# Two blocks of each Q head from exact codes, their scales applied inside Q's accumulator; a partition exchange by DMA; context rounding by an 8-bit store

## What is computed

```python
def _dequant(codes, scales):                       # codes 0..15, one scale per 128 rows and column
    w = codes.astype(jnp.float32) - 8.0
    return w * jnp.repeat(scales, GS, axis=0)      # GS = 128
q = hidden_states @ _dequant(q_codes, q_scales)    # 32 heads of 128; k, v: 8 heads
q = _rope(q); k = _rope(k)
attn = softmax(q @ k.T * HD ** -0.5 + causal_mask)
out = (attn @ v) @ _dequant(o_codes, o_scales)
def fake_quant(x, scale, zp):                      # for the context and for the normed x
    q = jnp.clip(jnp.round(x / scale + zp), 0.0, 255.0)
    return (q - zp) * scale
```

## Time and profile before

| | us |
|---|---|
| median of three runs (1077.76 to 1079.20) | 1079.08 |
| the profiled execution | 1078.07 |
| its span, first to last instruction | 1076.2 |
| PE, DVE, POOL, ACT busy in the span | 1034.3, 940.6, 785.6, 727.8 |
| K and V, before the first scores | 165.9 |
| slots 8 to 39 (context), start to start | 379.1 |
| slots 40 to 61, start to start | 259.3 |

### The profile page before, as it was taken

How to read it: one execution, slowest core, us unless ns; L and a number is a source line. 1 busy time by engine, 2 the same in 40 slices (tenths; PEclk the granted TensorE clock), 3 DMA queues, 4 the chain that set the end, 5 groups by cost and what they waited for, 6 DMA issues and landing times.

```text
span 1076.2 us, 19074 instructions
## 1 busy us (share of the span) xinstructions
PE 1034.3 (96%) x5356; PEld 503.9 (47%) x5356; DVE 940.6 (87%) x1741; ACT 727.8 (68%) x1589; POOL 785.6 (73%) x849
## 2 busy tenths in 40 slices
PE   5999998999999999999999999999999998989998
PEld 3444443444544454445445545544544453444443
DVE  7988998799888889888988889999999999878863
ACT  5547757767888888788878877777776776453320
POOL 4678888888888888788878888988888898332100
PEclk9999999999999999999999999999999999989999
DMA  9774303778667766666676666777776766423443
GB/s 340 246 189 131 110 20 83 154 146 163 166 147 165 157 151 151 160 161 153 153 156 157 154 152 152 160 150 153 158 165 148 151 128 130 119 83 64 98 103 79
DMA packets 309827, 156.13 MB, mean 145 GB/s; under 512 B 257728, under 2 KB 270400, under 8 KB 309728
## 3 DMA queue, kind: packets, MB, share of 16 engines
q1 hardware_dynamic: 301952, 141.69, 56.8%
q10 hardware_dynamic: 7776, 13.37, 3.9%
HBM read 89.20 MB, written 4.19 MB: 87 GB/s over the span
## 4 chain that ended last, share of the span: by engine, by line
POOL 49%; PE 18%; issue 17%; DVE 11%; ACT 2%; DMA 1%; POOLq 0%; DVEq 0%; SPq 0%; ACTq 0%
POOL w_b L1650 14%; POOL prob L1643 13%; POOL swapped L1638 7%; POOL rot L1658 4%; PE proj_ps L1107 4%; POOL q_sb L1663 3%; DVE rot L2018 2%; POOL ctx_raw L1771 2%; PE proj_ps L1112 2%; PE score_ps L1078 2%; POOL w_b L1744 2%; DVE x_acc L2113 1%; POOL rot L1686 1%; PE proj_ps L743 1%; PE proj_ps L744 1%
## 5 line engine op out<-in xcount | busy, mean ns | idle before, releaser
L1650 POOL TENSOR_TENSOR w_b<-prob,w_b 128x896 f16<-128x896 f32 (+2 forms) x192 | 188.6, 997 | 40.9 <-ACT w_b L1327 40.7
L1643 POOL TENSOR_SCALAR prob<-prob,row_inv 128x512 f32<-128x512 f32 (+3 forms) x256 | 166.8, 663 | 66.5 <-DVE row_inv L2191 60.8
L1300 ACT ACTIVATE prob<-score_ps,neg_max 128x512 f32<-128x512 f32 (+3 forms) x256 | 132.9, 522 | 74.5 <-DVE neg_max L2089 53.1
L745 PE MATMUL side_ps<-hT,w_a 128*128 128x512 f16 x444 | 168.3, 379 | 0.0
L744 PE MATMUL side_ps<-hT,w_a 128*128 128x512 f16 x444 | 168.3, 379 | 0.0
L743 PE MATMUL side_ps<-hT,w_a 128*128 128x512 f16 x444 | 168.3, 379 | 0.0
L2113 DVE SCALAR_TENSOR_TENSOR x_acc<-out_ps,o_now,x_acc 128x1024 f32<-128x1024 f32 x120 | 153.1, 1276 | 0.0
L2113 DVE SCALAR_TENSOR_TENSOR x_acc<-proj_ps,o_now,x_acc 128x1024 f32<-128x1024 f32 x120 | 152.6, 1272 | 0.0
L949 PE MATMUL proj_ps<-work,w_b 128*128 128x512 f16 x496 | 127.3, 379 | 4.7 <-issue 2.4
L949 PE MATMUL out_ps<-work,w_b 128*128 128x512 f16 x496 | 127.3, 379 | 0.9 <-DVE x_acc L2113 0.8
L2089 DVE CUSTOM_DVE_ANT_0 score_ps<-score_ps,mask_b 128x512 f32<-128x512 f32 (+3 forms) x256 | 121.7, 495 | 3.2 <-PE score_ps L912 3.1
(11 more groups left out here) (271 smaller groups left out, 2224.7 us busy)
## 6 DMA issues: line engine op xcount, KB each, us to landing
stage_c<-in_codes_dram SPq DMA_DIRECT2D x72, 256.0 KB, 2.9
stage_o<-in_codes_dram SPq DMA_DIRECT2D x64, 256.0 KB, 2.9
stage_s<-in_scales_dram SPq DMA_DIRECT2D x64, 256.0 KB, 3.5
ctx_raw<-in_ctx_dram ACTq DMA_DIRECT2D x32, 256.0 KB, 3.0
work<-w_b SPq DMA_TRANSPOSE x261, 3.1
x_acc<-in_x_dram SPq DMA_DIRECT2D x8, 512.0 KB, 8.4
k_sb<-in_codes_dram SPq DMA_DIRECT2D x16, 256.0 KB, 6.9
v_sb<-in_scales_dram SPq DMA_DIRECT2D x16, 256.0 KB, 7.3
```

Source lines behind the costliest of these rows:

```text
L745: return pe.matmul(o, stat(1), mov(0), start=False, stop=last)
L1300: ins = act.activation(prob[:, SCORE_AT[qb]:SCORE_AT[qb] + w], score_ps[:, score_bank(i, u), off:off + w], ACT.Exp, bias=neg_max[:, c:c + ...
L1643: return pool.tensor_scalar(prob[:, at:at + w], prob[:, at:at + w], row_inv[:, col:col + 1], P_UP, ALU.mult, ALU.mult)
L1650: ins = pool.tensor_tensor(prob16[:, 1, to:to + w], prob[:, at:at + w], prob16[:, 0, to:to + w], ALU.subtract)
```

## The change

1. Q's blocks 0 and 1 both come from exact codes (`N_EXACT = 2`), two matmuls each, into Q's own bank `q_ps`. ACT multiplies that bank in place after each of the two, first by the ratio of the two blocks' scales, then by block 1's scale; the other six blocks accumulate onto it. `q_join` is gone; PE waits for each of the two in-place multiplications. The codes of two blocks skip the work of splitting.
2. ACT copies Q out whole (`q_copy`) and SP exchanges the halves with two DMAs of 64 partitions (`swap_q`), queued ahead of the slot's four transposes. `q_swap` stays for the first four slots.
3. The context is scaled straight into 8-bit integers; POOL's clip and one of ACT's passes are gone.
4. The orders on PE, ACT, DVE and POOL are rewritten around this, and `scale_table` computes the ratios.

```diff
-EXACT = P
-EARLY = 2
+N_EXACT = 2
+EXACT = N_EXACT * P
-V_SLOTS = [(0, 2, 3, 5, 7), (7, 7, 8, 10, 12), (12, 12, 13, 16, 16)]
+V_SLOTS = [(0, 2, 3, 5, 7), (7, 7, 8, 10, 12), (12, 12, 15, 16, 16)]
+        ctx_codes = ctx_raw[:, 0:S // 4].bitcast(U8)
@@ SP
+            def swap_q(p):
+                sp.wait_ge(q_copied, p - FIRST_PIECES + 1)
+                for a in (0, 64):
+                    sp.dma_start(swapped[a:a + 64, :], q_sum_in[64 - a:128 - a, :]).then_inc(q_swap_landed, 16)
...
                         next_o(g, i)
+                    if by_parts(p + Q_AHEAD) and not (known(p) and p >= N_SLOTS - Q_AHEAD):
+                        swap_q(p + Q_AHEAD)
                     turn(p)
@@ PE
-                pe.wait_ge(piece_done, g * SLOTS + (2 * h + 2))
-                pe.wait_ge(ao_ready, p - 3)
+                if e:
+                    pe.wait_ge(q_based, 2 * (p - FIRST_PIECES) + 1)
+                else:
+                    pe.wait_ge(piece_done, g * SLOTS + (2 * h + 2))
...
+                        pe.wait_ge(q_copied, p - FIRST_PIECES)
+                w = (h % RING * KB + e) * P
                 for l in range(2):
-                    mm = pe.matmul(pv_ps, w_a[:, 0, h % RING * KB * P:(h % RING * KB + 1) * P],
-                                   hT[:, l, 0, i % B * S:(i % B + 1) * S], start=l == 0, stop=l == 1)
+                    mm = pe.matmul(q_ps, w_a[:, 0, w:w + P], hT[:, l, e, i % B * S:(i % B + 1) * S],
+                                   start=l + e == 0, stop=l == 1, skip_group_check=e > 0)
...
-                        pe.wait_ge(q_joined, p - FIRST_PIECES)
+                        pe.wait_ge(q_based, 2 * (p - FIRST_PIECES) + 2)
...
-                if not (known(p) and (p == 0 or p >= N_SLOTS - FIRST_PIECES + 1)):
-                    pe.wait_ge(q_based, p)
...
                 scores(p, i, g, 0)
+                if has_ahead and parts:
+                    q_exact(*ahead, 0)
                 if has_o and not (known(p) and p == O_LAG):
                     o_unit(p - 1, prev[1], 3)
                 scores(p, i, g, 1)
+                if has_ahead and parts:
+                    q_exact(*ahead, 1)
-                if has_ahead and parts:
-                    q_part(*ahead, range(1, EARLY))
                 if has_o:
                     o_unit(p, i, 0)
-                    q_exact(*ahead)
-                if has_ahead and parts:
-                    q_part(*ahead, range(EARLY, 3))
                 scores(p, i, g, 2)
+                if has_ahead:
+                    q_part(*ahead, range(N_EXACT if parts else 3, KB))
                 if has_o:
                     o_unit(p, i, 1)
-                if has_ahead:
-                    q_part(*ahead, range(3, KB))
-                if has_o:
                     o_unit(p, i, 2)
@@ ACT
+            def q_copy(p):
+                act.wait_ge(q_done, p + 1)
+                act.activation(q_sum_in, q_bank(p), ACT.Copy).then_inc(q_copied, 1)
-                act.activation(q_sum_in, pv_ps, ACT.Copy, scale=o_now[:, (i // B + 1) % 2, CB:CB + 1])\
+                act.activation(q_ps, q_ps, ACT.Copy, scale=o_now[:, (i // B + 1) % 2, CB + e:CB + e + 1])\
...
-                    act.activation(ctx_raw[:, :], ctx_raw[:, :], ACT.Identity, scale=scal[:, 5:6],
+                    act.activation(ctx_codes, ctx_raw[:, :], ACT.Identity, scale=scal[:, 5:6],
                                    bias=scal[:, 3:4]).then_inc(ctx_scaled, 1)
+                    act.activation(dst, ctx_codes, ACT.Copy, bias=-Q_MID).then_inc(ctx_free, 1)
@@ POOL
-                        sine(swapped[:, :], q_swapped, p + 1, q_sined)
                         q_turn(p + 1)
+                        sine(swapped[:, :], q_swap_landed, (p + 1 - FIRST_PIECES) * 32 + 31, q_sined)
-                        pool.tensor_scalar(ctx_raw[:, :], ctx_raw[:, :], QMAX, 0.0, ALU.min, ALU.max)\
@@ DVE
-                dve.tensor_tensor(q_sum_in, q_bank(p), q_sum_in, ALU.add).then_inc(q_joined, 1)
+                then_own(dve.tensor_tensor(by, rows[:, :, 1], rows[:, :, 1], ALU.mult))
+                then_own(dve.tensor_scalar(by, by, TINY * TINY, 2 * TINY, ALU.is_lt, ALU.mult))
+                then_own(dve.tensor_tensor(by, by, rows[:, :, 1], ALU.add))
+                then_own(dve.reciprocal(per, by))
+                then_own(dve.tensor_tensor(per, rows[:, :, 0], per, ALU.mult))
```

More of the change, by code:

```diff
@@ L740, in _, with three_products @@
         def _(pe):
-            def three_products(o, stat, mov, first, last):
-                pe.matmul(o, stat(0), mov(0), start=first, stop=False)
-                pe.matmul(o, stat(0), mov(1), start=False, stop=False)
-                return pe.matmul(o, stat(1), mov(0), start=False, stop=last)
+            def three_products(o, stat, mov, first, last, onto=False):
+                pe.matmul(o, stat(0), mov(0), start=first, stop=False, skip_group_check=onto)
+                pe.matmul(o, stat(0), mov(1), start=False, stop=False, skip_group_check=onto)
+                return pe.matmul(o, stat(1), mov(0), start=False, stop=last, skip_group_check=onto)
             def k_group(m, kb):
@@ L831, in q_part @@
                 p = g * SLOTS + i
-                first = 1 if by_parts(p) else 0
+                first = N_EXACT if by_parts(p) else 0
                 if known(p) and p < Q_AHEAD and kbs[0] % 4 == 0:
@@ L984, in slot @@
                 scores(p, i, g, 1)
+                if has_ahead and parts:
+                    q_exact(*ahead, 1)
                 if v_at:
                     v_blocks(v_at[2], v_at[3])
-                parts = by_parts(p + Q_AHEAD)
-                if has_ahead and parts:
-                    q_part(*ahead, range(1, EARLY))
                 if has_o:
                     o_unit(p, i, 0)
-                if has_ahead and parts:
-                    q_exact(*ahead)
-                elif has_ahead:
+                if has_ahead and not parts:
                     q_part(*ahead, range(0, 1))
-                if has_ahead and parts:
-                    q_part(*ahead, range(EARLY, 3))
                 scores(p, i, g, 2)
@@ L1383, in slot @@
                     act.dma_start(ctx_raw[:, :], tile.rearrange("a p n -> (a p) n")).then_inc(ctx_landed, 16)
+                if has_ahead and by_parts(p + Q_AHEAD):
+                    q_base(*next_q, 0)
                 if known(p) and p == 1:
@@ L1408, in slot @@
                     wf_sign(wf_early(p))
-                o_cut(p, i)
+                if has_ahead and by_parts(p + Q_AHEAD):
+                    q_copy(p + Q_AHEAD)
+                elif has_ahead:
+                    q_swap(p + Q_AHEAD)
+                if has_prev and known(p) and p < O_LAG:
+                    ao_part(p - 1, i - 1)
                 prob_split(p, 0)
-                if with_ctx:
-                    act.wait_ge(ctx_clipped, q + 1)
-                    act.activation(ctx_raw[:, :], ctx_raw[:, :], ACT.Copy, bias=ROUND).then_inc(ctx_rounded, 1)
-                if has_prev and not (known(p) and p == N_SLOTS - 1):
+                prob_split(p, 1)
+                if known(p) and p == N_SLOTS - 1:
+                    column_part(0, 0)
+                if not (known(p) and p < O_LAG):
                     ao_part(p - 1, (i - 1) % SLOTS)
-                if has_ahead:
-                    q_swap(p + Q_AHEAD)
-                if known(p) and p == N_SLOTS - 1:
-                    prob_split(p, 1)
-                    column_part(0, 0)
-                    ao_part(p - 1, i - 1)
-                    return
-                prob_split(p, 1)
-                if with_ctx:
-                    act.wait_ge(ctx_rounded, q + 1)
-                    act.activation(dst, ctx_raw[:, :], ACT.Copy, bias=-(ROUND + Q_MID)).then_inc(ctx_free, 1)
             def q_first(n):
@@ L2203, in slot @@
                     wf_difference(wf_early(p))
-                if has_ahead and by_parts(p + Q_AHEAD):
-                    q_join(p + Q_AHEAD)
                 if has_o:
+                    o_add(p, i, 1)
                     o_add(p, i, 2)
```

79 lines of the change are left out of this document (39 added, 40 removed).

## The result

The changed kernel takes 1080.95 us (median of 20 runs, 1078.19 to 1085.5) beside 1078.5 for the kernel before, run alongside it: a ratio of 1.0023, 95% interval 1.0015 to 1.0032. Forecast were 1063 and a range of 1056 to 1074. The columns did go; 18 us came back elsewhere.

The account below looks back on a forecast made before the run. PE was taken as the bound, with almost no idle. Terms -13.0 - 2.0 - 1.7 - 1.0 + 0.8 + 0.7 = -16.2 on the profiled 1078.07 gave 1061.9, with the median 1.0 higher about 1063 us; range 1056 to 1074.

Parts of the forecast that it names:

- main term: PE, slots with Q by parts: 60 matmuls fewer at 0.216 us each, -13.0 us; slot 53 units, 11.45 us.
- Third rival: Whole kernel: no change, 1078, because the loop through `prob` sets the period and PE has room; chance 0.05.
- The scaling in place: ACT, PSUM to PSUM on Q's bank: taken as 0.69 us each, from the same instruction into SBUF.
- second rival: In-place scaling on ACT takes 1.38 us, PE stalls in odd and even slots, kernel slower at 1088; chance 0.08.
- the thin cover: Odd context slots: second scaling just hidden from PE, so 0.05 us added in 16 slots, +0.8 us.
- It fits, barely: SP's queue, slots 40 to 61, with the exchange DMAs: 11.0 us of issues in a slot of 11.45.
- The landing at 7.4: Slots 40 to 61: last transpose lands at 7.4 us of the slot; `weigh` asks for it at 9.8.
- first rival's second mechanism: SP's queue stalls slots 40 to 61; that rival gave 1066 to 1074, say 1070, chance 0.21.
- Scale table: K's phase: eight small DVE instructions more at about 0.2 us each, 1.6 at most, 0 at least; +0.7 taken.
- these stay: Slots 8 to 39: some 3.3 of 6.0 us idle stand at the three loop turns and remain.
- idle that goes: PE idle time gained: 2.0 us in slots 8 to 39, 1.7 in slots 40 to 61, 1.0 in slot 62.
- fourth rival: More gained, 1055: all idle of slots 8 to 61 goes, loop turns too, and a shorter end; chance 0.09.

Follow-up runs that it names:

- experiment 9: Kernel before, with only ACT's loop over the context groups written out: 1072.05 us beside 1078.05, ratio 0.9954.
- experiment 12: Changed kernel with the scale table's ratio instructions spread over K, halves exchanged by ACT copies outside the loop, ACT's loop written out: 1059.49 us, ratio 0.9836.
- experiment 8: Kernel before with only the context rounded by conversion to 8 bits, POOL's clip left out: 1077.42 us beside 1077.43, ratio 1.0001.
- experiment 10: Changed kernel with one edit, halves exchanged by two ACT copies outside the loop instead of DMA: 1069.22 us, ratio 0.992.
- 13: Kernel of experiment 10 plus two DMAs nobody reads on SP's queue in each of slots 40 to 61: 1080.07 us, ratio 1.0015.
- Experiment 5: Changed kernel with ratio instructions spread, ACT's `ao_part` moved past the turn, exchange DMAs outside the loop issued by ACT right after `q_copy`: 1065.1 us, ratio 0.9884.
- experiment 3: Changed kernel with the exchange DMAs outside the loop issued by ACT, behind its last half of `prob`, not by SP: 1076.05 us, ratio 0.9988.
- 11: Kernel before plus two DMAs nobody reads on SP's queue in each of slots 40 to 61: 1079.41 us, ratio 1.0013.
- experiment 7: Kernel of 6 with ACT's loop over the context groups written out, other engines still looping: 1059.36 us, ratio 0.9834.
- experiments 1: Changed kernel with the scale table's five ratio instructions spread over later K turns: 1076.53 us, ratio 0.9989.
- 6: Changed kernel with ratio instructions spread, ACT's `ao_part` moved past the turn, halves exchanged by ACT copies outside the loop: 1064.55 us, ratio 0.988.

## Why the prediction was wrong

**What held.** *Bound and main term.* PE bounds slots 8 to 61, 54 units before and 53 after: 11.45 forecast, 11.46 measured in every slot in which nothing else is late. With the covers restored the stages are 366.7 and 252.2, which is 32 and 22 times 11.46. Timed on one chip, the kernel before and the changed one, both with ACT's loop written out and the latter with table and exchange mended (9 and 12), take 1072.05 and 1059.49: the change's own worth is 12.6 us. That it lies near the 13.0 of the 60 matmuls is in part luck: slots 8 to 61 give 14.4, more than their 54 matmuls (11.7), slot 62 and the end 2.2, and the start of slot 0 and slots 0 to 7 take 3.5 back (13.1 between the two profiled executions). *Third rival.* The rule on the LDWEIGHTS share, cited from the Trainium skill, Perfetto Trace Analysis, section Identifying the Most-Contended Engine, would have had PE with room at 47%. The trace disagrees: in experiment 12 that share is 51% in slots 8 to 61 (313.6 of 618.9 us), PE is busy for all of the 618.9, and each matmul less shortened the slot by 0.22. The same section names the share of peak FLOPs beside that of LDWEIGHTS; the prediction left it out. *The scaling in place.* Forecast 0.69, taken from the copy into SBUF; the page of after has 0.66 as the mean of 120. The second rival (1.38) has nothing for it, and there is no steady wait at either scaling, so the 0.8 for the thin cover did not come either: odd context slots take 11.46 like even ones. The Trainium skill, ScalarE: Activation LUTs, section ACT is a hardware spline evaluator, has writes to PSUM faster than to SBUF, and 0.66 against 0.69 agrees. *Rounding:* nothing, experiment 8. *Slot 62:* -1.6 for -1.0.

**What failed, in order of size.**

1. *"It fits, barely"* (SP's queue in slots 40 to 61): 9.1 us between forecast and result, the main error. The step that failed is the sum of 11.0 us of issues for 11.45: over the stage the queue's work was 11.6 a slot, in the slot shown 11.76. The sum took four transposes at 1.3 each and left out the 0.05 between these issues; the row it went by had the four at 7.18, and in the slot shown they took 5.79. At 11.6 the queue doesn't fit, and none of its waits, 7.0 us, is made up: 22 times 0.14 and 7.0 are some 10 us. The landing at 7.4, for 9.8, supposed that the transposes start at 0.3 of the slot, where they started at 2.7. It was the first rival's second mechanism, named at 1066 to 1074 and priced too low. Experiments 10 and 13 show it from both sides: without the exchange on the queue 252.2, with two idle DMAs in its place 261.0. Experiment 5 leaves the exchange a DMA but takes it off SP's queue: 254.0.

2. *Scale table, 0.7 with a bound of 1.6:* 5.3, of which 3.7 are PE's pause and some 1.7 the lower clock behind it, which the prediction looked for only behind slot 63. The price of 0.20 came from a row in which POOL was idle; beside a POOL instruction the same kind of row lasts up to 1.3. The upper bound was no bound, because it was made of the same row. And K's own loop was no cover, since PE's waits in K's phase are all for DVE, which was busy 59.8 of 64 us there before the change (102 to 166 us).

3. *Loop turns, "these stay":* slots 8 to 39 gained 3.4 less than forecast. A slot got shorter and the jump did not: 13.3 against 11.46 is 1.8 a turn, where 12.7 to 12.9 against 11.7 was 1.0 to 1.2. That makes 2.1. The other part is slots 8 to 10 (12.2, 12.6 and 11.8), SP's queue again after the work on wf in the slots up to 7; they are back at 11.46 in experiment 3. That makes 2.2; the other idle time went by 0.9 more than forecast.

4. *Slots 0 to 7, not costed apart:* +1.0 for the -1.3 of six matmuls; 0.7 of it in slots 2 to 7. PE waits 0.8 once for a scaling, and the exponentials are later. Copies instead of the exchange do not mend it (95.6). Why the exponentials are later there stays open.

Most of the 18 us are thus three covers that the change used up and that the forecast had called sufficient. The first forecast gain, "idle that goes", was in the end there too: all idle time of slots 8 to 61 can go, but only when ACT's jump and SP's load go first. So the fourth rival (1055) was the better guide to what the change could give: 1059.5 with the covers restored, some 20 us below the changed kernel by the ratios (0.9836 and 1.0023). Part of that, about 6 us, the kernel before can have too, by writing out ACT's loop (experiment 9).

## What to carry to other kernels

Where a change moves work from an engine to a queue, compare the queue's work per period with the new period, the time between issues included, and take the lengths from the row in which it is busiest. Here a queue that still waited 12% of the stage cost nothing (experiment 10); with 3% it cost 0.7 us in the kernel before (11) and with 2.5% 8.8 in the shorter slots (13); no run shows what lies between. Two idle DMAs are a cheap trial, but at the old pace they show little: it is the shorter slot that they have to fit. Take the price of a small DVE instruction from a row beside a busy POOL, not from one beside an idle one. And look at what stands right behind a loop's jump on each engine: a shorter period makes the same jump more visible.

## What the runs showed of the hardware

- *A DVE TENSOR_TENSOR or TENSOR_SCALAR of 3 to 32 columns can last until POOL's instruction beside it is over:* in the changed kernel 1.19, 0.76 and 1.19, ending 0.04 to 0.05 after POOL's. In experiment 12 the five at a K turn of their own took 1.28, 1.29, 1.28, 0.34 and 1.26; the four long ones also end 0.04 to 0.08 behind a POOL instruction. The short one is the RECIPROCAL, which in both kernels lies wholly beside a POOL instruction and is not held. That POOL blocks them is read from these ends; a kernel with POOL idle there was not tried.
- *The end of ACT's loop* leaves 2.2 us from the end of its last instruction to the next issue. Written out, it is gone (experiment 7), and that gains 6 us even in the kernel before (experiment 9), about half of it at the turns.
- *The same two DMAs* on one queue cost 0.7 us in 22 slots of 11.8 where the queue had 39 us of waits, and 8.8 in slots of 11.46 where it had 30.
- *PE's granted clock* was 0.50 from 95.8 to 99.1 us, after PE had stood 3.7 us (0.88 as a mean over 88 to 102), 0.88 again in experiment 10, which has the same table, and 1.00 there in the kernel before and in experiments 1, 6 and 7, where PE does not stand.
